# Gathering q and v separately: the scores pass gathers q rows, the attention sums gather v rows by edge

## The reference

```python
q = (feat @ Wq.T + bq).reshape(n, H, D)
k = (feat @ Wk.T + bk).reshape(n, H, D)
v = (feat @ Wv.T + bv).reshape(n, H, D)
e = jnp.einsum('ehd,ehd->eh', q[src], k[dst]) * scale
m = jax.ops.segment_max(e, dst, num_segments=n)
ex = jnp.exp(e - m[dst])
denom = jax.ops.segment_sum(ex, dst, num_segments=n)
sa = ex / denom[dst]
agg = jax.ops.segment_sum(sa[:, :, None] * v[src], dst, num_segments=n)
```

## Time and profile before

| | |
|---|---|
| time of the runs, us | median 3722.77 (3722.48 to 3745.7, 3 runs) |
| the profiled execution, us | 3709.9, of it span 3708.2 |
| PE busy in the span | 3001.6 us (81%) |
| DVE busy | 2103.5 us (57%) |
| POOL busy | 1144.1 us (31%) |
| ACT busy | 1116.2 us (30%) |
| DMA | 477.29 MB, mean 129 GB/s |
| mean granted TensorE clock | 0.893 |

### The profile page before, as it was taken

How to read it: one execution, slowest core, us unless ns; L and a number is a source line. 1 busy time by engine, 2 the same in 40 slices (tenths; PEclk the granted TensorE clock), 3 DMA queues, 4 the chain that set the end, 5 groups by cost and what they waited for, 6 DMA issues and landing times. The chain is left out here.

```text
span 3708.2 us, 59832 instructions
## 1 busy us (share of the span) xinstructions
PE 3001.6 (81%) x12443; PEld 2281.0 (62%) x12444; DVE 2103.5 (57%) x3955; ACT 1116.2 (30%) x2514; POOL 1144.1 (31%) x1249
## 2 busy tenths in 40 slices
PE   3766566656399969999996999999997995748978
PEld 2643344433255647777774888888886874535567
DVE  6356555556699554544422665656669985881221
ACT  1010111100388413334331000000008965643212
POOL 3155555554022010000001555555550005620023
PEclk9877777776699879999997999999998997979979
DMA  1587777787477320000002665666650113005234
GB/s 48 176 252 217 228 221 230 232 238 200 131 227 227 94 69 1 8 1 8 8 8 76 191 189 176 191 180 189 190 165 22 43 43 118 1 0 206 85 127 136
DMA packets 236310, 477.29 MB, mean 129 GB/s; under 512 B 30380, under 2 KB 121460, under 8 KB 234796
## 3 DMA queue, kind: packets, MB, share of 16 engines
q1 hardware_dynamic: 175150, 282.91, 23.9%
q0 software_dynamic: 61056, 193.06, 18.2%
HBM read 376.68 MB, written 100.16 MB: 129 GB/s over the span
## 5 line engine op out<-in xcount | busy, mean ns | idle before, releaser
L1664 PE MATMUL bank<-conv_w,conv_eT 128*128 128x256 f32 x2520 | 580.7, 380 | 0.0
L1664 PEld LDWEIGHTS bank<-conv_w,conv_eT 128*128 128x128 f32 x2520 | 480.8, 191 | 66.1
L1605 POOL DMA_INDIRECT conv_h<-table_h,conv_ix x424 | 416.8, 983 | 334.7 <-ACT conv_ix L1594 192.3
L557 POOL DMA_INDIRECT x<-table_qv,scores_ix x324 | 307.2, 948 | 383.4 <-ACT scores_ix L505 266.5
L579 PE MATMUL bank<-scores_k,scores_hotT 128*128 x864 | 326.6, 516 | 56.6 <-issue 50.6
L1397 ACT ACTIVATE area<-bank,nodes_bi,nodes_sc 128x320 f32<-128x320 f32 x320 | 197.6, 617 | 375.3 <-PE bank L1314 375.3
L579 PEld LDWEIGHTS bank<-scores_k,scores_hotT 128*128 128x128 f32 x864 | 205.0, 257 | 135.0 <-issue 104.7
L1545 DVE SCALAR_TENSOR_TENSOR x<-bank,nodes_w,x 128x256 f32<-128x256 f32 x200 | 96.6, 484 | 321.2 <-PE bank L1323 321.2
L1045 PE MATMUL bank<-attend_pv,rows 128*128 128x260 f32 x864 | 237.0, 403 | 36.8 <-DVE attend_pv L1026 21.4
L571 PE MATMUL bank<-lines,pick 128*128 x216 | 73.8, 342 | 233.8 <-DVE scores_hotT L662 145.3
L1594 ACT ACTIVATE conv_ix<-src 128x2 int32 x212 | 43.2, 204 | 720.6 <-issue 558.5
(11 more groups left out here) (436 smaller groups left out, 5459.6 us busy)
## 6 DMA issues: line engine op xcount, KB each, us to landing
conv_eT<-in_edges SPq DMA_DIRECT2D x212, 384.0 KB
attend_v<-edge_v SPq DMA_DIRECT2D x216, 256.0 KB, 3.0
edge_v<-x SPq DMA_DIRECT2D x162, 256.0 KB
edge_v<-scores_qv SPq DMA_DIRECT2D x54, 256.0 KB
hidden_rows<-rows SPq DMA_DIRECT2D x25, 512.0 KB, 3.9
projected<-spline_hst SPq DMA_DIRECT2D x10, 960.0 KB, 4.6
ball_hT<-projected SPq DMA_DIRECT2D x5, 1920.0 KB, 17.5
top_wd<-in_top_wd SPq DMA_DIRECT2D x8, 1024.0 KB, 11.8
```

The costliest lines, as they stand in the source:

```text
L557: nc.gpsimd.indirect_dma_start(out=qv(u)[:, g - u * G, :], out_offset=None, in_=m.d_qv, in_offset=bass.IndirectOffsetOnAxis(ap=ix[:, g:g + ...
L1605: nc.gpsimd.indirect_dma_start(out=h[:, u, g, :], out_offset=None, in_=m.d_h, in_offset=bass.IndirectOffsetOnAxis(ap=ix[:, u * G + g:u * G ...
L1664: mm = nc.tensor.matmul(banks[u][:, g * F:(g + 1) * F], eT[:, u, g, c], w[:, c], start=c == 0, stop=c == EC - 1)
```

## The change

The tables are now three: q, k and v, rows of 1 KB each. The scores pass gathers q rows only (1 KB) and stores nothing: SP's loop of waits and stores is gone, and with it POOL's wait on `stored`. In the attention sums SP's loop of v loads is gone. POOL copies the source numbers of each step into a small index tile (`source`), waits for its own copy, and gathers v rows of 1 KB with two indirect DMAs a step (`gather`), four steps ahead of the step whose probabilities it copies (`probs`); each round of 8 steps is written out in the order source(u + 5), probs(u), gather(u + 4). `source` waits until DVE has read the ring's buffer (`weighted`). DVE waits for both gathers of a step instead of one load.

```diff
@@ -436,9 +436,7 @@
     with Stage(nc, "scores") as st:
         k = st.sb("k", [P, NT, F])
         ix = st.sb("ix", [P, RING * G], I32)
-        in_x = NT * F // (G * 2 * F)
-        qv_x = m.x[:].rearrange("p t f -> p (t f)")[:, 0:in_x * G * 2 * F].rearrange("p (u g f) -> p u g f", u=in_x, g=G)
-        qv_more = st.sb("qv", [P, RING - in_x, G, 2 * F])
+        q = m.x[:].rearrange("p t f -> p (t f)")[:, 0:RING * G * F].rearrange("p (u g f) -> p u g f", u=RING, g=G)
         hotT = st.sb("hotT", [P, UN, G * P])
         qk = st.sb("qk", [P, 2, G * F])
         dot = st.sb("dot", [P, 2, G, HEADS])
@@ -456,40 +454,19 @@
                                 "front_made", "ekv_kept", "back_made"))
         tiled = st.sem("tiled")
         steps_saved = st.sem("steps_saved")
-        k_loaded, gathers, seen = st.sem("k_loaded"), st.sem("gathers"), st.sem("seen")
-        stored = [st.sem(f"stored{u}") for u in range(RING)]
+        k_loaded, gathers = st.sem("k_loaded"), st.sem("gathers")
         gathered = [st.gather_sem(f"gathered{g}") for g in range(RING * G)]
 
         def numbers(u):
             return banks[UN + u % 2][:, 0:G * P]
 
-        def qv(u):
-            return qv_x[:, u] if u < in_x else qv_more[:, u - in_x]
         with nc.Block() as block:
             @block.sync
             def _(sp):
-                for u in range(RING):
-                    sp.sem_inc(stored[u], 16)
                 sp.dma_start(k[:], m.d_k.rearrange("(t p) f -> p t f", p=P)).then_inc(k_loaded, 16)
                 sp.dma_start(wk, a["mix_wk"]).then_inc(w_loaded, 16)
                 sp.dma_start(wv, a["mix_wv"]).then_inc(w_loaded, 16)
                 sp.dma_start(m.d_steps, m.steps).then_inc(steps_saved, 16)
-                rounds = rounds_of(sp, m, RING)
-                with sp.Fori(0, rounds) as r:
-                    for u in range(RING):
-                        t, i = step_at(sp, m, r * RING + u)
-                        for g in range(G):
-                            sp.wait_ge(gathered[u * G + g], r * 16 + 16)
-                            sp.sem_inc(seen, 1)
-                        if u < UN:
-                            sp.wait_ge(stored[u + UN], r * 16 + 16)
-                        else:
-                            sp.wait_ge(stored[u - UN], r * 16 + 32)
-                        sp.sem_inc(seen, 1)
-                        sp.dma_start(m.d_v[u % UN][:, bass.ds(i, G), :], qv(u)[:, :, F:2 * F]).then_inc(stored[u], 16)
-                for u in range(RING):
-                    sp.wait_ge(stored[u], rounds * 16 + 16)
-                    sp.sem_inc(seen, 1)
                 sp.wait_ge(steps_saved, 16)
 
             @block.scalar
@@ -551,11 +528,10 @@
                 with pool.Fori(0, rounds_of(pool, m, RING)) as r:
                     for u in range(RING):
                         pool.wait_ge(index, r * RING + (u + 1))
-                        pool.wait_ge(stored[u], r * 16 + 16)
                         pool.sem_inc(gathers, 1)
                         for g in range(u * G, (u + 1) * G):
                             nc.gpsimd.indirect_dma_start(
-                                out=qv(u)[:, g - u * G, :], out_offset=None, in_=m.d_qv,
+                                out=q[:, u, g - u * G, :], out_offset=None, in_=m.d_q,
                                 in_offset=bass.IndirectOffsetOnAxis(ap=ix[:, g:g + 1], axis=0)
                             ).then_inc(gathered[g], 16)
 
@@ -666,7 +642,7 @@
                         dve.wait_ge(gathered[g], r * 16 + 16)
                     dve.wait_ge(k_made, r * RING + (u + 1 + UN))
                     dve.wait_ge(reduced, r * RING + (u + 1))
-                    nc.vector.tensor_tensor(qk[:, u % 2].rearrange("p (g f) -> p g f", g=G), qv(u)[:, :, 0:F],
+                    nc.vector.tensor_tensor(qk[:, u % 2].rearrange("p (g f) -> p g f", g=G), q[:, u],
                                             banks[u % UN][:, 0:G * F].rearrange("p (g f) -> p g f", g=G), ALU.mult).then_inc(freed, 1)
                     if u + 2 < RING:
                         one_hot(r, u + 2)
@@ -901,13 +877,15 @@
     with Stage(nc, "attend") as st:
         v = st.sb("v", [P, RING, G, F])
         pv = st.sb("pv", [P, RING, G, WIDE])
+        ix = m.rows[:].rearrange("p t f -> p (t f)")[:, RING * G * P:RING * G * (P + 1)].bitcast(I32)
         minus = st.sb("minus", [P, ET])
         far = st.sb("far", [P, RING, G * P])
         hot = m.rows[:].rearrange("p t f -> p (t f)")[:, 0:RING * G * P].rearrange("p (u n) -> p u n", u=RING)
         weighted, multiplied, kept, hots, copied, own = (
             st.sem(x) for x in ("weighted", "multiplied", "kept", "hots", "copied", "own"))
         diff, exps, free, x_loaded = st.sem("diff"), st.sem("exps"), st.sem("free"), st.sem("x_loaded")
-        arrived = [st.sem(f"arrived{u}") for u in range(RING)]
+        index = st.sem("index")
+        arrived = [st.gather_sem(f"arrived{g}") for g in range(RING * G)]
         with nc.Block() as block:
             @block.sync
             def _(sp):
@@ -920,12 +898,6 @@
                 sp.dma_start(m.vec[:, 7], a["gnn1_bnode"]).then_inc(x_loaded, 16)
                 sp.dma_start(m.bgate[:], a["gnn_bgate"]).then_inc(x_loaded, 16)
                 sp.dma_start(m.slope[:], a["gnn_slope"]).then_inc(x_loaded, 16)
-                with sp.Fori(0, rounds_of(sp, m, RING)) as r:
-                    for u in range(RING):
-                        t, i = step_at(sp, m, r * RING + u)
-                        sp.wait_ge(weighted, r * RING + (u + 1))
-                        sp.sem_inc(free, 1)
-                        sp.dma_start(v[:, u], m.d_v[u % UN][:, bass.ds(i, G), :]).then_inc(arrived[u], 16)
                 sp.wait_ge(x_loaded, 16 * 15)
 
             @block.scalar
@@ -970,13 +942,47 @@
                 pool.sem_inc(hots, RING)
                 pool.sem_inc(weighted, RING)
                 pool.sem_inc(kept, RING)
+
+                def source(r, u):
+                    t, i = step_at(pool, m, r * RING + u)
+                    pool.wait_ge(weighted, r * RING + (u + 1))
+                    nc.gpsimd.tensor_copy(ix[:, u * G:(u + 1) * G], m.src[:, bass.ds(i, G)]).then_inc(index, 1)
+
+                def gather(r, u):
+                    pool.wait_ge(index, r * RING + (u + 1))
+                    pool.sem_inc(free, 1)
+                    for g in range(u * G, (u + 1) * G):
+                        nc.gpsimd.indirect_dma_start(
+                            out=v[:, u, g - u * G, :], out_offset=None, in_=m.d_v,
+                            in_offset=bass.IndirectOffsetOnAxis(ap=ix[:, g:g + 1], axis=0)
+                        ).then_inc(arrived[g], 16)
+
+                def probs(r, u):
+                    t, i = step_at(pool, m, r * RING + u)
+                    pool.wait_ge(multiplied, r * RING + (u + 1))
+                    nc.gpsimd.tensor_copy(pv[:, u, :, F:WIDE], m.probs[:, bass.ds(i, G), :]).then_inc(copied, 1)
+                AHEAD = 4
+                for u in range(AHEAD + 1):
+                    source(0, u)
+                for u in range(AHEAD):
+                    gather(0, u)
                 pool.wait_ge(exps, 1)
-                with pool.Fori(0, rounds_of(pool, m, RING)) as r:
+                last = last_round(pool, m, RING)
+
+                def round_of(r, more):
                     for u in range(RING):
-                        s = pool.snap(r * RING + u)
-                        t, i = step_at(pool, m, s)
-                        pool.wait_ge(multiplied, s + 1)
-                        nc.gpsimd.tensor_copy(pv[:, u, :, F:WIDE], m.probs[:, bass.ds(i, G), :]).then_inc(copied, 1)
+                        if u + AHEAD + 1 < RING:
+                            source(r, u + AHEAD + 1)
+                        elif more:
+                            source(r + 1, u + AHEAD + 1 - RING)
+                        probs(r, u)
+                        if u + AHEAD < RING:
+                            gather(r, u + AHEAD)
+                        elif more:
+                            gather(r + 1, u + AHEAD - RING)
+                with pool.Fori(0, last) as r:
+                    round_of(r, True)
+                round_of(last, False)
 
             @block.vector
             def _(dve):
@@ -990,7 +996,8 @@
 
                 def weigh(r, u, word):
                     i = edge_tile(dve, word)
-                    dve.wait_ge(arrived[u], r * 16 + 16)
+                    for g in range(u * G, (u + 1) * G):
+                        dve.wait_ge(arrived[g], r * 16 + 16)
                     dve.wait_ge(multiplied, r * RING + (u + 1))
                     nc.vector.tensor_tensor(pv[:, u, :, 0:F].rearrange("p g (h d) -> p g h d", h=HEADS),
                                             v[:, u].rearrange("p g (h d) -> p g h d", h=HEADS),
@@ -1022,7 +1029,8 @@
                     dve.reg_mov(carried[k], word)
                     if k < 2:
                         i = edge_tile(dve, word)
```

(8 more changed lines are left out.)

## The result

The changed kernel takes 4127.2 us (median of 4 runs, 4115.8 to 4150.8) beside 3722.9 us: 1.108 times the time before, 95% interval 1.102 to 1.114. The forecast was 3959 us with a range to 4110: the direction was right and the time lay 17 us above the range.

A forecast was written before the change was run, and what follows sets the result against it. The prediction took DVE, slowed by sequencer stalls, to pace the scores pass and TensorE to bound the sums. Saving 185 us and losing 421 gave +236 on 3722.8, so 3959 us, range 3865 to 4110.

The forecast's parts named there:

- the saving of 185 us in the scores pass: Scores pass: a step falls from 3.50 to 2.62 us, saving 185 us, with ends at 125 and 209.
- the load of wide gathers makes the stalls: Scores pass: 2 KB gathers make DVE's sequencer instructions take up to 717 ns, so a step costs 3.5 instead of 2.3 us.
- absent wherever gathers are narrow: Argument against stalls remaining in the scores pass: DVE's sequencer shows none in the convolution (1 KB gathers) or the sums (none).
- POOL as the bound of a pass without stalls, 2.51 us a step: Scores pass: two gathers of 1.255 us each set a floor of 2.51 us a step, 542 us.
- stalls stay: Rival: something left in the scores pass causes the stalls, a step stays 3.5 us, nothing saved, 4144 us; chance 0.10.
- 3.20 us a step: Attention sums: POOL's two gathers and two index or probability copies take 3.20 us a step, between 2.89 and 3.49.
- 421 us of loss: Attention sums: bound by POOL, they end at 1667 instead of 1246, a loss of 421 us (354 to 484).
- POOL's sequencer runs ahead: Attention sums: POOL's register loads and waits, 2.5 us a step, hide under its 3.2 us of work.
- POOL held by DVE's products: Rival: in the sums each DVE product holds a POOL instruction 0.69 us, 149 us more, 4108 us; chance 0.03.
- Lock-step: Rival: in the sums each POOL load, copy and gather waits for the last, 4.44 us a step, 4227 us; chance 0.05.
- faster: Rival: gathers' 1.255 us is back-pressure; scores pass at 2.3, sums at 1.9 us a step, 3609 us; chance 0.03.

The follow-up runs named there:

- half_rows: Kernel after, each gather of the scores pass fetching 64 rows instead of 128 (the other partitions constant); 4106.3 us.
- after_fill384: Kernel after with one POOL memset of 128x384 behind each scores gather, 1.55 us gather to gather; 4008.0 us beside 3504.8 of the kernel before.
- hwload: Kernel after, q rows of the scores pass fetched by SP with plain DMAs from fixed rows instead of POOL's gathers; 3860.3 us beside 3700.5 of before.
- nogather: Kernel after, POOL filling the q buffers of the scores pass with constants (memsets of 128x256) instead of gathering; 3865.9 us beside 3697.5 of before.
- the group at 3505 us: Group of four runs with slower or half-row scores gathers, beside which the unchanged kernel before took 3505 us instead of 3695 to 3727.
- before_fill384: Kernel before with one POOL memset of 128x384 behind each scores gather, 1.55 us gather to gather; 3615.7 us beside 3694.7 of before.
- before_r4: Kernel before with the scores pass in rounds of 4 steps instead of 8; 3734.6 us, ratio to before 1.009.
- after_r4: Kernel after with the scores pass in rounds of 4 steps instead of 8; 4124.3 us, ratio to before 1.117.
- pace2: Kernel after with two POOL memsets of 128x8 behind each scores gather, 1.27 us gather to gather; 4090.9 us beside 3700.5 of before.

## Why the prediction was right and wrong

**Its failed step is the saving of 185 us in the scores pass.** It rested on one inference, that the load of wide gathers makes the stalls, since the convolution's narrow ones do without on DVE. The pass gave -11 instead of +185, 196 us of the 205 by which the span's difference (441) missed the forecast 236. More than the width of the row differed between the two stages: the pace of issue did, 1.25 us in the pass in a row and 1.77 in the convolution on the mean. It could be read from the earlier trace rows and I used it only for POOL's price. And the earlier trace rows look at DVE alone. SP's step words in the convolution of the kernel before, with its narrow gathers, show the same stalls, 29 in all on SP there, so "absent wherever gathers are narrow" was false on the trace at hand:

```profile
L400 SPq FUSED_REGOPS  x159: 3/51/713, 2020.3 to 2760.0; - x159
```

The runs show that the width has no part in it (`half_rows`, `after_fill384`), nor the traffic (`hwload`), that POOL's gathers have (`nogather`), and that in one group of runs 1.55 us between them was enough to be rid of the stalls on DVE and TensorE. What in the indirect DMAs holds the sequencers stays open. The bound for this step was set from 125 to 209 us of saving, none of it at nothing; that is why the range ended below the time.

**Even right, the step would have been wrong.** Where there are no stalls, the kernel before does not have them either (by its 3505 us, not by a trace), and its pass is near POOL's 540 us too. The forecast compared a kernel before with stalls with a kernel after without. The state of the sequencers was treated as part of the kernel; the group at 3505 us shows that it is not of the kernel alone.

**POOL as the bound of a pass without stalls, 2.51 us a step.** Shown by `before_fill384` for its own pace, and by subtraction (552 us) for the bare one. It was not seen in a trace of the unchanged kernel.

**The rival "stalls stay" came true in its time**, 4144 forecast and 4127 measured, with a chance of 0.10. The reasons that it named did not: the loop is not the cause (`before_r4`, `after_r4`), nor are the index copies, which `nogather` and `hwload` keep. What stays in the pass and makes the stalls are the 432 gathers themselves.

**The sums: 3.20 us a step forecast, 3.08 measured; 421 us of loss forecast, 404 measured.** Two gathers are 2 x 1.050 = 2.10 us instead of 2.51 + 0.07 - 0.60 = 1.98 without gaps; the idle time before them is 102.9 / 216 = 0.48 instead of 0.60, since the first gather behind a copy waits only 0.16; the two copies are 0.52 instead of 0.53; and the gap before them, which I set from 0 to 0.60 and took at 0.09, is none. That POOL's sequencer runs ahead held.

**The rival "POOL held by DVE's products"** is half true. In most steps one gather or copy starts under the product and is longer for it, 1.48 against 0.95 us above. The Trainium skill, "SBUF — State Buffer", section "Who interferes with whom", says that a DVE instruction with two SBUF inputs contends with a GpSimd instruction that reads SBUF, over a lock that one of them holds; the trace agrees. But the sum already held three fifths of it (gathers 2 x 35 ns, the copies' mean 264 instead of 191 ns), and its whole is (2 x 102 + 100 + 46) ns = 0.35 us a step, 76 us, not 149 on top. The 102, 100 and 46 are the means 1050, 293 and 226 of gather and copies over their medians 948, 193 and 180.

**Not foreseen:** 18 us behind the sums. The stretch from 1661 to 2473 shows the same matmuls at a clock of 0.90 instead of 0.92, after a stage in which TensorE sat at 0.50 instead of 0.99. And 10 us in the convolution, whose SP sequencer had 50 slow register operations instead of 29; their number does not explain the time (`after_r4`, with 11, had gathers over 761.9 us there, `pace2`, with 31, over 750.0), and the cause stays open.

**Lock-step and "faster"** did not come: the second copy starts at the first one's end or before it, and no gather of the two passes took less than 940 ns.

## What to carry to other kernels

An indirect DMA on GpSimd had a price in issues here, about 0.95 us of POOL and 0.30 us before it, whether the row was 2 KB or 1 KB; cutting the row in half saved bytes and no time, and splitting one gather of two things into two gathers doubled the price. Before a stage is said to gain from a stall that vanishes, change what is thought to cause it in a run of its own: two stages that differ in the stall differ in more than one thing, and the stages that you leave alone tell in the same trace whether the stall could have come at all. And when a stall has no releaser in the profile, keep zero as an end of the range, and look whether the kernel before has it in each group of runs.

No version here is safely better than the kernel before: `before_fill384` was 2.1% faster while there were stalls (one run, 3615.7 beside 3694.7) and 2.8% slower when there were none.

## What the runs showed of the hardware

- Indirect DMAs issued by POOL in a row, 1.25 us apart, go with single register operations of 0.7 us on the sequencers of DVE, TensorE and SP in the scores pass (ACT's step-word operations never over 51 ns there), and on POOL (90), ACT (44) and DVE (20) in the sums of the kernel after. The scores pass cost 3.5 us a step with them and 2.33 without gathers; the sums, bound by POOL, took as long with them as without (gathers over 651.6 to 664.6 us, and 653.9 and 663.8).
- Neither the bytes (128 rows of 2 KB, 128 of 1 KB, 64 of 1 KB) nor the length of the loop changes that; as many rows of 1 KB fetched by SP with plain DMAs make none (2.33 us a step).
- A slower issue does: 80 slow operations on DVE at 1.44 us, none at 1.55 and at 1.66, within one group of runs and in executions whose other stages had stalls. SP still had 7 at 1.55. That something drains in between is a guess; no run shows it.
- It comes and goes from outside the kernel: the same program took 3941.9 and 4115.3 us, the kernel before 3505 and 3727 us. Why is open too. The condition was the same in all traces of a group: slow operations in each, or none in any. One candidate was not tried: the Trainium skill, "NOTIFIC — the notification-queue block", section "Overflow: three behaviours, one of which stalls the engine", says that this block, which writes out the engines' records, holds its producers rather than lose one inside. No run here shows whether the recording has a part in these stalls.
- More work on POOL can shorten a stage: one memset of 0.43 us behind each gather took DVE's products in the pass of the kernel before from 730 to 655 us, while there were stalls; without them it made that kernel 2.8% slower.
